# A focused-attention and mixture-of-experts kernel: row maxima written at 16 bits into the transposed stack, a first copy moved to ScalarE, half of the key masks moved to GpSimd

## The reference

```python
def step(carry, i):
    qcur, prev, attn, cw, temp, done = carry
    qp = qcur @ lq_w.T + lq_b
    sq = _ln(qp, lnc_w) * tscale
    sk = _ln(k_full @ lk_w.T + lk_b, lnd_w)
    scores = einsum('bhqd,bhkd->bhqk', sq, sk) * inv_sqrt_e
    in_win = pos < cw
    scores = where(in_win[None, None, None, :], scores, -inf)
    probs = softmax(scores, axis=-1)
    out = einsum('bhqk,bhkd->bhqd', probs, vp)
    iter_out = where(in_win[None, None, :, None], out, 0.0)
    diff = mean(abs(iter_out - prev))
    ...
    up, down = int(cw * 1.1), int(cw * 0.9)
    nw = where(diff > 0.05, up, where((diff < 0.001) & (cw > 64), down, cw))
```

## Time and profile before

| what | value |
|---|---|
| runs, us | 392.17, 392.46, 394.63 |
| median, us | 392.46 |
| the profiled execution, us | 395.93 |
| its span, first to last instruction, us | 394.2 |
| granted TensorE clock, mean over the span | 0.795 |
| busy: PE, DVE, ACT, POOL (share of the span) | 74%, 74%, 44%, 47% |

### The profile page before, as it was taken

The page is one execution under the profiler, slowest core; times in us unless marked ns, Lnnn a source line. Parts: engine busy times, 40 slices in busy tenths (PEclk is TensorE's granted clock), DMA queues, the critical chain, the costliest instruction groups (busy, mean ns, idle before and its releaser), DMA issues.

```text
span 394.2 us, 7916 instructions
## 1 busy us (share of the span) xinstructions
PE 291.2 (74%) x2211; PEld 221.1 (56%) x2212; DVE 289.8 (74%) x855; ACT 174.4 (44%) x356; POOL 184.5 (47%) x317
## 2 busy tenths in 40 slices
PE   1692888767952778969679999979967903999950
PEld 1482326523231231459679999967456802999940
DVE  7678999999578999278866676625798594688840
ACT  1213593215830228965334555544536620555510
POOL 8574486580057660002377445545135762245550
PEclk9877568555795556989999999989997555899995
DMA  3299999993011112011123222167900223233310
GB/s 88 29 342 331 336 375 373 377 375 106 2 35 48 41 54 30 2 28 40 42 76 64 78 70 65 32 175 235 284 2 3 95 79 91 56 94 100 86 40 0
DMA packets 45442, 47.09 MB, mean 119 GB/s; under 512 B 11614, under 2 KB 29619, under 8 KB 45409
## 3 DMA queue, kind: packets, MB, share of 16 engines
q1 hardware_dynamic: 41424, 39.21, 32.8%
q0 software_dynamic: 3936, 7.49, 6.1%
q10 hardware_dynamic: 48, 0.00, 0.0%
HBM read 19.50 MB, written 28.09 MB: 121 GB/s over the span
## 4 chain that ended last, share of the span: by engine, by line
PE 41%; DVE 33%; issue 7%; ACT 5%; POOL 4%; DMA 4%; SPq 2%; DVEq 0%; POOLq 0%; ACTq 0%
PE ps L1407 12%; PE ps L1418 11%; DVE mx L2030 10%; PE ps L1235 3%; ACT wide L884 2%; PE ps L1218 2%; POOL rows L654 2%; DMA rows<-token_rows,posu 2%; SPq L317 2%; PE ps L1257 2%; PE ps L1391 1%; DVE ps L2291 1%; DMA xs<-rows 1%; DMA small<-in_L_attn_lnd_w 1%; PE ps L1472 1%
## 5 line engine op out<-in xcount | busy, mean ns | idle before, releaser
L666 POOL DMA_INDIRECT back<-ys,places x39 | 38.7, 991 | 68.8 <-DVE ys L2176 63.2
L654 POOL DMA_INDIRECT rows<-token_rows,posu x48 | 47.9, 997 | 42.8 <-DVE posu L1931 22.4
L1418 PE MATMUL ps<-w_out,hg 128*128 x496 | 66.1, 278 | 0.3 <-DVE ys L2176 0.3
L1418 PEld LDWEIGHTS ps<-w_out,hg 128*128 128x128 f32 x496 | 60.9, 194 | 0.6 <-issue 0.4
L982 ACT ACTIVATE hg<-hb 128x512 f32<-128x512 f32 x62 | 39.1, 630 | 39.3 <-DVE hb L2165 33.4
L2165 DVE TENSOR_TENSOR hb<-ps,b_in 128x512 f32<-128x512 f32 x62 | 42.5, 686 | 13.8 <-PE ps L1407 13.6
L2030 DVE TENSOR_REDUCE mx<-ps 128x2 f32<-128x562 f32 (+2 forms) x64 | 43.1, 740 | 0.7 <-PE ps L1199 0.6
L1407 PE MATMUL ps<-xsT,w_now 128*128 128x128 f32 x256 | 38.7, 299 | 5.0 <-DVE hb L2165 2.6
L866 ACT COPY qs<-ps 128x768 bf16<-128x768 bf16 (+1 forms) x21 | 15.3, 730 | 55.5 <-PE ps L1178 55.5
L1407 PEld LDWEIGHTS ps<-xsT,w_now 128*128 128x128 f32 x256 | 34.8, 211 | 6.2 <-issue 5.1
L666 POOL DMA_INDIRECT out<-ys,rest x23 | 22.7, 988 | 32.6 <-DVE ys L2184 27.0
(11 more groups left out here) (424 smaller groups left out, 589.4 us busy)
## 6 DMA issues: line engine op xcount, KB each, us to landing
rows<-blank SPq DMA_DIRECT2D x73, 260.0 KB, 6.4
xs<-rows SPq DMA_DIRECT2D x62, 64.0 KB, 1.8
w_in<-in_L_ffn_w_fc SPq DMA_DIRECT2D x1, 2048.0 KB, 12.1
w_in<-in_L_ffn_W SPq DMA_DIRECT2D x1, 2048.0 KB, 11.0
rest<-rows SPq DMA_DIRECT2D x23, 65.0 KB, 1.9
token_rows<-in_L_attn_x SPq DMA_DIRECT2D x1, 832.0 KB, 8.3
wmod<-in_L_wmod SPq DMA_DIRECT2D x2, 384.0 KB, 4.5
rows<-token_rows,posu POOLq DMA_INDIRECT x48, 2.4
```

The costliest lines, as they stand in the source:

```text
L654: pool.indirect_dma_start(ROWS[l], bass.IndirectOffsetOnAxis(ap=posu[:, k, j:j + 1], axis=0), token_rows[:, j, 0:WIDTH[l]], None).then_inc ...
L666: pool.indirect_dma_start(where, bass.IndirectOffsetOnAxis(ap=target[r] if l else places[:, t, :].bitcast(U32)[:, 0:1], axis=0), ys[:, r, ...
L1418: mm = pe.matmul(ps[:, 6 + c % 2, 0:D], hg[:, c % RING, n * P:(n + 1) * P], w_out[:, bass.ds(e * NB + n, 1), :], start=(n == 0), stop=(n = ...
```

## The change

- `mx` is gone. The reduces write their two maxima straight into slot 1 of `stack`, converted to bf16, and the twelve copies of L2023 go. TensorE's turns of the maxima wait for the reduces themselves. The memset of `mx` on GpSimd, which also gave `max_free` a head start of 2, goes, and the waits count 2 less.
- In passes 1 and 2 the first copy is made by ScalarE, behind its other work and ahead of its copies of the other quarters. In pass 0 VectorE still makes it.
- In passes 1 and 2 GpSimd writes the masks of heads 4 to 15, two instructions in a row, the second waiting for the first. In pass 1 this stands ahead of the doubling of 256 columns, in place of the wait for the queries; in pass 2 it stands behind the eleventh of the 26 sends and waits until those eleven have landed.

```diff
+MASK_AT = 11
...
-        mx = sb("mx", [P, NA, HEADS])
...
-            pool.memset(mx[:], 0.0).then_inc(sem("max_free"), 2)
...
+            def mask_keys(it):
+
+                nw = WINDOWS[it]
+                pool.wait_ge(sem("ks_set"), 2 * it - 1)
+                for p0 in (0, STK):
+                    ins = pool.tensor_scalar(ks[p0:p0 + 1, 2:HEADS // 2, WMIN:nw], kidx[p0:p0 + 1, WMIN:nw].unsqueeze(1).to_broadcast([1, HEADS // 2 - 2, nw - WMIN]),
+                                             cw[p0:p0 + 1, it:it + 1], MASKED, ALU.is_ge, ALU.mult)
+                    if p0 == 0:
+                        then(ins)
+                ins.then_inc(sem("ks_set"), 1)
+                pool.wait_ge(sem("ks_set"), 2 * it)
+
             for m in range(NPOW - 2):
                 if m == NPOW - 4:
 
-                    pool.wait_ge(sem("q_stack"), 2)
+                    mask_keys(1)
...
                 for j in range(NA, NT):
+                    if sent == MASK_AT:
+                        pool.wait_ge(sem("scattered_far"), 16 * (sent - sent // 2))
+                        pool.wait_ge(sem("scattered_odd"), 16 * (sent // 2))
+                        mask_keys(2)
                     if sent > 1:
...
+                if it:
+                    act.wait_ge(sem("stackT"), 8 * it + 1)
+                    act.copy(qs[:, 0:2, 0:blocks(it) * P], turned(0, 6, blocks(it) * P)).then_inc(sem("qs_first"), 1)
                 for step in (1, 2, 3):
                     stack_copy(it, step)
...
-                        if U0 + u:
-                            pe.wait_ge(sem("max_free"), U0 + u)
+                        if U0 + u > 2:
+                            pe.wait_ge(sem("max_free"), U0 + u - 2)
...
-                    pe.wait_ge(sem("max_stack"), G0 + g + 1)
+                    pe.wait_ge(sem("max_free"), U0 + 2 * nj * (g + 1))
...
-                            pe.wait_ge(sem("max_free"), U0 + units + u)
+                            pe.wait_ge(sem("max_free"), U0 + units + u - 2)
...
-                def stack_maxima(g):
-
-                    v.wait_ge(sem("max_free"), 2 + U0 + 2 * nj * (g + 1))
-                    v.tensor_copy(stack[:, 0:nj * HEADS, 1].rearrange("p (j h) -> p j h", h=HEADS)[:, :, 4 * g:4 * g + 4],
-                                  mx[:, 0:nj, 4 * g:4 * g + 4]).then_inc(sem("max_stack"), 1)
-
...
-                    b = score_bank(it, u)
+                    b, at = score_bank(it, u), j * HEADS + 2 * p
                     v.wait_ge(sem("s_ready"), U0 + u + 1)
-                    v.tensor_reduce(mx[:, j, 2 * p:2 * p + 2], ps[:, b:b + 2, 0:nw], AX.X, ALU.max).then_inc(sem("max_free"), 1)
-                    if u % (2 * nj) == 0 and u:
-                        stack_maxima(u // (2 * nj) - 1)
-                stack_maxima(3)
+                    v.tensor_reduce(stack[:, at:at + 2, 1], ps[:, b:b + 2, 0:nw], AX.X, ALU.max).then_inc(sem("max_free"), 1)
...
-                    first_copy(it, nj)
                     window_of(it)
                     if it == 1:
                         v.wait_ge(sem("ks_masked"), 2)
                     mask_keys(it, 0, 2)
-                    mask_keys(it, 2, HEADS // 2)
```

## The result

| | before | after |
|---|---|---|
| median of 20 runs each, us | 392.89 | 389.36 |
| ratio, 95% interval | | 0.992, 0.9896 to 0.9945 |
| the profiled execution, us | 395.93 | 392.27 |

The change takes 3.1 us off by the ratio (2.2 to 4.1), 3.5 by the medians; 3.9 was forecast. The ratios are worked out from the fast runs and are not the quotients of the medians, from which they differ by up to 0.9 us (e6). Runs of one kernel spread over some 5 us, so the stages of the traces say more than the totals. The profiled execution before, 395.93, is slower than each of the twenty runs (391.26 to 395.55), so the difference of the two profiles, 3.7, is no measure of the change either.

A forecast was written before the change was run, and what follows sets the result against it. VectorE's path through the maxima was taken to bound the passes. Savings of 0.27, 2.45 and 1.19 us in passes 0, 1 and 2 made 3.9, taking the median from 392.46 to 388.5; 8-in-10 range 387.0 to 391.8.

The forecast's parts named there:

- The copies: VectorE's copies of the maxima: removing those inside the reduces saves 0.19, 1.40 and 0.19 us in passes 0, 1 and 2.
- The copy behind pass 0: Last copy of the maxima in pass 0, between VectorE's reduces and its next work: removing it saves 0.08 us.
- A reduce that writes bf16: VectorE's reduces writing two bf16 maxima: no extra cost taken, bounded below 0.02 us each, 1.3 over 64.
- The first copy: Lead-in of passes 1 and 2: moving it to ScalarE is worth nothing; VectorE's wait for TensorE becomes 0.72 us.
- The leads: Before the first reduce: masks leaving VectorE save 0.88 us in pass 1 and 1.00 in pass 2, L1999 0.17 more.
- The masks in time: GpSimd's masks, 1.35 and 1.86 us each, ready for unit 6 with 1.1 and 0.4 to spare; counted at nothing.
- The formula of the rival: Stall before unit 6 if masks come late: 3.72r + 127.94 - 132.08 in pass 2, r being GpSimd's rate over L733's.
- late masks: Rival: GpSimd's masks miss unit 6 and VectorE stalls; late but still a gain 0.16, slower than before 0.06.
- late but still a gain: Case of masks missing unit 6 with the kernel still faster; at r = 1.2 it costs 0.3 us; chance 0.16.
- The caught rowm: Rival: in passes 1 and 2 VectorE's rowm waits behind GpSimd's first mask; gain only 1.4 us, 391.1; chance 0.08.
- The work moved on GpSimd: Doublings some 6 us later in pass 1, fifteen sends 6 us later in pass 2, last near 152; all covered.
- TensorE's clock: Rival: behind the maxima the clock rises 2 us sooner or later, moving a pass about 1 us; chance 0.10.

The follow-up runs named there:

- e6: Kernel before with one wait changed: GpSimd starts the doublings of 256 and 512 columns behind the maxima of pass 1; 391.06 us against 391.94 (1.0002).
- e1: Kernel before with only the edits to the reduces of the maxima and their waits, so the twelve copies go; 388.65 us against 392.0 (0.992).
- e3: Whole change with the first copy of passes 1 and 2 back on VectorE; 385.97 us against 392.0 for the kernel before (0.9875).
- e7: Kernel before with seven extra GpSimd instructions of 612 numbers behind the doublings, writing memory nobody reads; ran once, 392.35 us.
- e11: Second run of the kernel before with only the edits to the reduces of the maxima and their waits; 388.32 us against 391.88 (0.9918).
- e5: Whole change with each of GpSimd's mask instructions issued twice, writing the same values; 397.81 us against 391.94 for the kernel before (1.015).
- e2: Kernel before with only the masks of heads 4 to 15 moved to GpSimd, all copies staying on VectorE; 390.19 us against 392.0 (0.9964).
- e10: Second run of the whole change with the first copy of passes 1 and 2 back on VectorE; 387.56 us, 0.9899 of the kernel before.
- e4: Whole change with GpSimd's masks in two separately signalled parts, heads 4 to 7, then 8 to 15; 387.01 us against 392.0 for the kernel before (0.9889).
- e8: Whole change, unaltered, run again on another chip; 389.5 us against 391.88 for the kernel before (0.9953).
- e9: Second run of the whole change with GpSimd's masks in two separately signalled parts; 390.42 us against 391.88 for the kernel before (0.9938).
- e12: Whole change with GpSimd's masks in two parts and the first copy of passes 1 and 2 on VectorE; 387.87 us against 391.17 before (0.9907).

## Why the prediction was right, and where it was off

**The copies.** Right in all three passes inside the reduces: 0.21, 1.40 and 0.21 (0.19, 1.40, 0.19 forecast), by e1. That GpSimd made two of them dear is shown by e6, where they took 0.18. The copy behind pass 0 was priced too low: 0.08 was forecast, from the end of the reduces to the next work, but that work now starts 0.08 ahead of the end of the last reduce (49.48 for 49.56). From there to the output it is 13.99 instead of 14.22, so pass 0 gained 0.44 and not 0.27.

**A reduce that writes bf16.** Right in the sum: 0.65 from one to the next in pass 1, as before. The single instruction is longer by some 0.01 (medians of 739 for 727 ns in pass 1, 797 for 790 in pass 2), hidden where they run back to back.

**The first copy.** Right in the passes: e3 has the same leads. VectorE's wait grew from 0.16 to 0.75 without the copy, where 0.72 was forecast.

**The leads.** 1.23 and 0.99 measured (13.77 to 12.54, 14.69 to 13.70) against 1.05 and 1.00 forecast. The first reduce followed the first scores by 0.52 and 0.55, as pass 0 had suggested. Of the 0.18 more in lead 1, 0.06 is L1999, now L2018, which took 0.16 where I had put 0.22; another 0.06 lies between the start of the first masks and TensorE's first scores (0.70 for 0.76), and the rest ahead of VectorE's wait for the change.

**The masks in time.** This step failed in pass 2. I took 1.86 for a mask of 612 numbers, by proportion from L733, which does one operation; the mask does two and took 2.37 (r = 1.27); e7 shows the second operation to be the cause. The formula of the rival, with that price, gives a stall of 2 x 2.37 + 127.94 - 132.08 = 0.60, and the profile shows 0.58. So the frame held and one price was wrong. The forecast had named the second operation among the reasons for late masks, gave "late but still a gain" 0.16, and set the sum without it. With 0.68 more in reduces 2 the forecast's sum would be 3.2. That this stands beside 3.1 by the ratio is partly luck. The stages that the change moves gave 0.44 in pass 0, 1.23 + 1.40 in pass 1 and 0.99 - 0.47 in pass 2, together 3.6, as the terms put too low (pass 0, lead 1) stand against the stall; the ratios say 3.1 on one chip and 1.8 on the other, whose interval holds neither 3.2 nor 3.6. The profiles differ by 3.8 in their spans: 3.6 less in these stages, 0.5 more in the rests, 0.9 less in the tail, 0.2 more ahead of pass 0. In pass 1 the masks took 1.81 each against 1.35, inside its 1.1 to spare.

**The caught rowm.** It did not happen: rowm ran from 75.50 to 75.73 and took no longer (0.23, 0.25 before) though GpSimd's mask started at 75.64. It was ahead by 0.14, and in no trace does the mask come first. The mask is a tensor_scalar, beside which VectorE lost 0.4 at most elsewhere, where the rival put 1.35.

**The work moved on GpSimd.** Right: first send 2.9 sooner (106.96 for 109.83), last send at 152.83, "near 152", and the masks of pass 2 began with VectorE's signal. The doublings ended at 93.9, and one instruction of the choice of experts took 1.13 beside their last tensor_tensor, inside VectorE's slack (2.87 at 99.95). e6 shows how close that was: with the doublings 13.6 us later than in the kernel after the same kind of collision ate 1.4 us. The price of this cover should have been in the forecast, which spoke only of GpSimd's own wait.

**TensorE's clock.** Granted clock in the stretches behind the maxima of pass 1, of the whole change and of e11 (columns as in rows 10):

```profile
91.80:101.00 9.20, 8.27 (x62) 2.13 (x62) 5.71 (x21) 7.66 (x15) 2.00 (x2) 0.50 0.07 23
101.00:111.80 10.80, 10.43 (x118) 4.81 (x110) 8.43 (x38) 7.61 (x16) 3.19 (x3) 1.00 0.07 21
```

```profile
92.60:94.20 1.60, 1.55 (x12) 0.85 (x12) 1.43 (x6) 1.60 (x5) 0.00 (x0) 0.50 0.09 30
94.40:110.60 16.20, 14.63 (x161) 6.12 (x160) 11.74 (x52) 13.06 (x26) 3.29 (x3) 1.00 0.05 16
```

With the whole change the clock stayed at 1.2 GHz for 9.3 us behind the last reduce, until 101.08, and the rest took 20.03; in e11 it rose after 1.7 and the rest took 18.07. The other traces stand between. The time from the last reduce to the rise, beside the rest, in us:

| pass 1 | rise | rest | | pass 2 | rise | rest |
|---|---|---|---|---|---|---|
| e11 | 1.7 | 18.07 | | e11 | 6.5 | 20.01 |
| e1 | 5.9 | 18.98 | | e1, e7 | 6.6 | 20.07, 20.10 |
| e5 | 6.1 | 19.02 | | e2, e3 | 7.0 | 20.11, 20.13 |
| e7 | 6.3 | 19.14 | | e10 | 7.3 | 20.24 |
| e3, e4 | 6.6, 6.7 | 19.26, 19.27 | | before | 7.6 | 20.38 |
| e10 | 7.0 | 19.42 | | e8 | 7.7 | 20.43 |
| e9, e12 | 7.4 | 19.62, 19.61 | | e6, e4 | 7.8 | 20.48, 20.50 |
| e8 | 7.8 | 19.78 | | e9, e12 | 8.1, 8.2 | 20.60, 20.61 |
| before | 8.3 | 19.93 | | e5 | 8.7 | 20.75 |
| whole change | 9.3 | 20.03 | | whole change | 9.0 | 20.74 |
| e2 | 7.7 | 20.11 | | | | |
| e6 | 6.6 | 21.35 | | | | |

So the scatter of the rests is the clock, to some hundredths, whatever the edit. Between 6 and 8.5 a microsecond of delay costs 0.34 to 0.4 us, less below and above; the forecast put 0.5 (1 us for 2 us). Two rows lie off. In e2, some 0.35 above the others, the last copy of the maxima took 1.32 (92.64), so that copy is on the path when it is held. In e6, 2.1 above them, VectorE came 2.2 late to the output. It is the mechanism that the forecast named, and it accounts for rest 1 in e1 and e11.

The tail has it in part. The whole change was profiled twice, with tails of 226.4 and 223.3. In the first the clock fell back to 1.2 GHz from 193.2 to 196.6 and again from 217.1 to 220.5, with TensorE busy for 77% of the stretch ahead of the first (172.9 to 193.1) and 81% ahead of the second (196.8 to 217.0); in e8 it held (columns as in rows 10, the first from the whole change, the second from e8):

```profile
193.30:196.60 3.30, 3.30 (x18) 3.30 (x17) 2.49 (x6) 1.32 (x4) 2.45 (x3) 0.50 0.19 60
...
217.20:220.40 3.20, 3.20 (x17) 3.20 (x17) 1.41 (x3) 1.12 (x3) 0.98 (x1) 0.50 0.16 46
```

```profile
169.80:292.40 122.60, 108.25 (x863) 98.46 (x861) 86.92 (x258) 60.84 (x122) 57.83 (x76) 1.00 0.34 95
```

At these two places VectorE's timeline of the first falls behind that of e8 by another 0.9 and 1.7 us. That is not the whole of it (the tail of e1 is 2.5 longer than that of e6 with the clock low for about as long), and how much of the 2 us between the whole change and the versions with the copy on VectorE is such scatter is open.

## What to carry to other kernels

Before work is given to another engine, price it by an instruction with the same number of operations on that engine, and set it against the time at which its first reader needs it: 0.42 us to spare on 3.72, or 11%, was not enough for a price taken from a like instruction. If only part of the work is needed first, signal that part by itself (e4). A wait changed on one engine moves its collisions with others: e6 took 1.7 us off the lead and the maxima and lost most of it to the same doublings 20 us later. Where runs spread over 5 us, judge a part by the stages of the trace that should move, not by totals, and compare a stage that TensorE bounds at the same granted clock.

## What the runs showed of the hardware

- On GpSimd a tensor_scalar of 612 numbers took 1.80 us with one operation and 2.34 with two, with one operation the same for 1 and 128 partitions and for f32 and bf16 out (e7).
- One VectorE instruction ahead of pass 0, the first of the root (L1647 before, L1666 after), took 1.52 us in the profile after and 0.18 in that of e8, the same kernel. Ten of the fourteen traces have such a long one (in e1 it is the instruction just before the root, 1.58), four have none. The first reduce stood at 39.3 to 39.9 with it and at 38.1 to 38.3 without. Every later time shifts with it, so it is part of the spread.
- Three of GpSimd's indirect sends took 2.82, 1.89 and 1.73 instead of 0.97 while VectorE multiplied w_out and b_out and later the rotations. In the kernel before they had gone ahead of that work. There was room for it here.
- The length of TensorE's work behind the maxima followed the time at which the granted clock rose, in all traces but two that have another cause (the table above).
- VectorE's small instructions with operands in SBUF waited up to 1.1 us for GpSimd's tensor_tensors (1.32 for 0.18, e2; 1.35 for 0.27, e6) and 0.4 at most for its tensor_scalars. The reduces from PSUM did not wait: those of pass 1 took 724 to 744 ns before, with the doublings beside part of them, and 728 to 743 in e6, with GpSimd idle. The Trainium skill has this as a lock (page SBUF — State Buffer, section "SBUF: two separate sides"): whoever starts first holds the shared ports for its whole instruction. The waits behind the tensor_tensors are as long as what was left of them, so the traces agree there; for the tensor_scalars they do not show it.
